# Batch 14's rotation and the first weight split on the other side of a stage boundary, and three scale loads in the attention

## The reference

```python
x = x + jnp.tanh(g_xattn[0]) * _L0_xattn_ref(_layernorm(x, axis=-1), ctx_2048, ctx_2048)
x = x + jnp.tanh(g_ffn[0]) * _L0_ffn_ref(_layernorm(x, axis=-1), L0_ffn_SU_ug, L0_ffn_SU_dp, ...)
...
# _L0_ffn_ref, SCALE = 64, INTER = 2048
x = fwht(x * SU_ug) / SCALE
x_up = x @ W_up.T * (Wscale_ug[:INTER] * SCALE)
x_gate = x @ W_gate.T * (Wscale_ug[INTER:] * SCALE)
x = jax.nn.silu(x_gate) * x_up
x = fwht(x * SU_dp) / SCALE
x = x @ W_down.T * (Wscale_dp * SCALE)
```

## Time and profile before

| what | value |
|---|---|
| median of 3 runs | 2079.65 us (2076.43 to 2081.3) |
| profiled execution | 2077.13 us, span 2075.4 us |
| PE busy | 2005.1 us (97%) |
| DVE, ACT, POOL busy | 1238.7, 1159.2, 825.6 us |
| mean granted clock of TensorE | 0.986 |

### The profile page before, as it was taken

How to read it: one execution, slowest core, us unless ns; L and a number is a source line. 1 busy time by engine, 2 the same in 40 slices (tenths; PEclk the granted TensorE clock), 3 DMA queues, 4 the chain that set the end, 5 groups by cost and what they waited for, 6 DMA issues and landing times. The chain is left out here.

```text
span 2075.4 us, 37475 instructions
## 1 busy us (share of the span) xinstructions
PE 2005.1 (97%) x13368; PEld 1677.3 (81%) x13368; DVE 1238.7 (60%) x2346; ACT 1159.2 (56%) x3063; POOL 825.6 (40%) x997
## 2 busy tenths in 40 slices
PE   8999999999989999999979997899999999899998
PEld 6877777777768888898868886899999999778886
DVE  6766666666644543565445555666666666466665
ACT  5666666666643333353333345777777777355544
POOL 3526436445321000000003445888888787022222
PEclk9999999999999999999999998999999999999999
DMA  5536446454275210203003435333333333311101
GB/s 178 151 96 191 121 132 203 120 153 142 86 216 194 79 61 1 71 1 117 1 26 107 121 116 147 87 96 99 114 97 107 98 104 89 120 57 52 31 28 37
DMA packets 199368, 210.08 MB, mean 101 GB/s; under 512 B 65677, under 2 KB 139853, under 8 KB 198685
## 3 DMA queue, kind: packets, MB, share of 16 engines
q1 hardware_dynamic: 199197, 207.83, 33.1%
HBM read 128.13 MB, written 79.66 MB: 100 GB/s over the span
## 5 line engine op out<-in xcount | busy, mean ns | idle before, releaser
L1815 POOL TENSOR_TENSOR qd_rows<-qd_rows,c_rsum 112x375 f32<-112x375 f32 x256 | 202.2, 811 | 90.2 <-DVE c_rsum L1945 83.2
L1951 DVE TENSOR_TENSOR c_pT_lo<-c_turned,c_pT_hi 125x336 fp32r<-125x336 f32 x256 | 128.4, 502 | 135.2 <-ACT c_pT_hi L1890 135.0
L1881 ACT ACTIVATE qd_rows<-c_score,c_nmax 112x375 f32<-112x375 f32 x256 | 147.1, 575 | 86.7 <-DVE c_nmax L1940 86.7
L1262 ACT ACTIVATE b_silu<-b_gate,b_ug_scale 128x512 f32<-128x512 f32 (+1 forms) x64 | 40.7, 636 | 245.9 <-PE b_up L1384 245.8
L1323 DVE SCALAR_TENSOR_TENSOR b_hidden<-b_up,b_ug_scale,b_silu 128x512 f32<-128x512 f32 (+1 forms) x64 | 43.7, 683 | 197.9 <-ACT b_silu L1262 197.9
L518 ACT ACTIVATE a_probs<-a_score,a_nmax 112x375 f32<-112x375 f32 x256 | 144.5, 575 | 3.1 <-DVE a_nmax L678 3.0
L2229 POOL TENSOR_TENSOR f_probs<-f_probs,f_rsum 112x448 f32<-112x448 f32 x64 | 59.7, 933 | 212.1 <-DVE f_rsum L2350 212.1
L928 PEld LDWEIGHTS a_turned<-keep_ident,a_probs 112*125 112x125 f32 x768 | 110.4, 188 | 35.5 <-issue 22.6
L1940 DVE TENSOR_REDUCE c_nmax<-c_score 112x1 f32<-112x375 f32 x256 | 137.5, 537 | 0.4 <-PE c_score L2021 0.4
L928 PE MATMUL a_turned<-keep_ident,a_probs 112*125 112x112 f32 x768 | 133.8, 283 | 1.5 <-DVE a_pT L684 1.0
L1241 POOL TENSOR_TENSOR ab_zT<-ab_zT,keep_ln_eps 128x1 f32<-128x1 f32 x1 | 0.2, 189 | 310.5 <-DVE ab_zT L1352 310.5
(11 more groups left out here) (335 smaller groups left out, 6079.6 us busy)
## 6 DMA issues: line engine op xcount, KB each, us to landing
q<-q_qT SPq DMA_DIRECT2D x14, 1024.0 KB
qd_raws<-q SPq DMA_DIRECT2D x64, 224.0 KB, 4.5
k<-bq_raw SPq DMA_DIRECT2D x16, 752.0 KB, 4.1
qd_raws<-k SPq DMA_DIRECT2D x64, 188.0 KB, 3.3
v<-bq_raw SPq DMA_DIRECT2D x48, 250.0 KB
qd_raws<-v SPq DMA_DIRECT2D x64, 187.5 KB
bq_raw<-in_ctx_dram SPq DMA_DIRECT2D x15, 672.0 KB
wug<-a_ug_turned SPq DMA_DIRECT2D x32, 256.0 KB, 2.3
```

Of the source, the lines that this page charges most:

```text
L1815: pool.tensor_tensor(probs[:, n % AHEAD, :], probs[:, n % AHEAD, :], rsum[:, n % (2 * H):n % (2 * H) + 1].broadcast_to([S, T]), ALU.mult). ...
L1881: act.activation(probs[:, n % AHEAD, :], score[n % AHEAD][0:S, 0:T], ACT.Exp, bias=nmax[:, c:c + 1], accum_out=sums[:, c:c + 1]).then_inc( ...
L1951: dve.tensor_tensor(pT[1][:, t % 2, :, j, :], src, f32(pT[0][:, t % 2, :, j, :]), ALU.subtract).then_inc(pT_split, 1)
```

## The change

The tail of phase_a no longer turns, copies, rotates, splits and stores batch 14. In phase_b TensorE starts with the four transposes of its z (into `y[3]`), ACT copies them after its first weight split, TensorE multiplies by the Hadamard matrix behind `project(0)` (into `y[2]`), ACT and DVE split the result within step 0, and `reduce(0)` waits for that. SP stores it after all weights, ahead of `load_turned(1)`. The split of weight chunk 0 moves from phase_b into phase_a's tail (b = 16, n = 0), on ACT ahead of `keys_out(15, 2)`, on DVE ahead of `gated(15)`. The buffers `wu` and of the scales move into `ab`. The three scale loads move into phase_a, at b = 8, behind `load_first` and ahead of batch 9's list. The diff, cut to its core:

```diff
             def load_first():
...
+            def load_scales():
+                with nc.allow_non_contiguous_dma(reason="scales by partition"):
+                    sp.dma_start(ab["ug_scale"][:, :], io["Wscale_ug"].rearrange("(c p) -> p c", p=P)).then_inc(ab["scales_loaded"], 16)
+                    sp.dma_start(ab["down_signs"][:, :], io["SU_dp"].rearrange("(c p) -> p c", p=P)).then_inc(ab["scales_loaded"], 16)
+                row = io["Wscale_dp"].rearrange("(a n) -> a n", a=1)
+                sp.dma_start(ab["down_scale"][:, :], row.broadcast_to([P, D])).then_inc(ab["scales_loaded"], 16)
...
-                if b >= 2:
+                if 2 <= b < B:
                     store_rotated(b - 2)
                 if b == B // 2:
                     load_first()
+                    load_scales()
...
+            for n in range(2):
+                sp.wait_ge(lead_loaded[n], 32)
+            sp.wait_ge(ab["scales_loaded"], 48)
...
+            def lead_weights_hi():
+                act.wait_ge(lead_loaded[0], 32)
+                act.activation(ab["wu"][0][:, 0, :, :, :], lead_weights, ACT.Copy).then_inc(lead_hi, 1)
...
+                    if n == 0 and b == B:
+                        lead_weights_hi()
                     if n == 0 and before:
                         keys_out(b - 1, 2)
...
-                    if n == 5 and b >= 2:
+                    if n == 5 and b >= 2 and cur:
                         copy_z(b - 2)
...
+                    if n == 0 and b == B:
+                        dve.wait_ge(lead_hi, 1)
+                        dve.tensor_tensor(ab["wu"][1][:, 0, :, :, :], lead_weights, f32(ab["wu"][0][:, 0, :, :, :]), ALU.subtract)
                     if n == 1 and before:
                         gated(b - 1)
...
-            with nc.allow_non_contiguous_dma(reason="scales by partition"):
-                sp.dma_start(ug_scale[:, :], ...
             for c in range(LEAD, 4):
                 load_weights(c)
...
             load_x(0)
+            sp.wait_ge(early_split, 1)
+            store_rotated(final - 1)
             load_turned(1)
...
-            for t in range(2):
-                weights_hi(t)
-            act.wait_ge(scales_loaded, 48)
+            weights_hi(1)
+            act.wait_ge(early_turned, 1)
+            act.activation(zT[:, :], y[3][:, 0:DC * S], ACT.Copy).then_inc(early_copied, 1)
...
+                if t == 0:
+                    act.wait_ge(early_rotated, 1)
+                    act.wait_ge(ab["xr_stored"], 32 * (final - 1))
+                    act.activation(xr[0][:, :, :], y[2][:, 0:DC * S].rearrange("p (c s) -> p c s", c=DC), ACT.Copy,
+                                   scale=float(D) ** -0.5).then_inc(early_hi, 1)
...
+            for c in range(DC):
+                last = pe.transpose(y[3][:, c * S:(c + 1) * S], z[:, 0, c * P:(c + 1) * P], keep["ident"][0:S, 0:S])
+            last.then_inc(early_turned, 1)
             project(0)
+            pe.wait_ge(early_copied, 1)
+            pe.matmul(y[2][:, 0:DC * S], keep["hadamard"][:, :], zT[:, :], start=True, stop=True).then_inc(early_rotated, 1)
```

More of the change, by code:

```diff
@@ L136, in first_layer @@
             "xr": [m.sb(f"xr_{n}", [P, DC, S], F32R) for n in ("hi", "lo")],
+            "wu": [m.sb(f"wu_{n}", [P, 2, 2, DC, P], F32R) for n in ("hi", "lo")],
+            "down_scale": m.sb("down_scale", [P, D]),
+            "down_signs": m.sb("down_signs", [P, IC]),
+            "ug_scale": m.sb("ug_scale", [P, 2 * IC]),
             "v_stored": [m.sem(f"v_stored{n}") for n in range(KC)],
         }
-        for name in ("x_stored", "k_stored", "xr_stored", "xres_loaded"):
+        for name in ("x_stored", "k_stored", "xr_stored", "xres_loaded", "scales_loaded"):
             ab[name] = m.sem(name)
@@ L205, in phase_a @@
         kout = stage[:, STAGE_V:].rearrange("p (c t) -> p c t", c=DC)
+        lead_weights = ab["lead"][:, B % CTX, 0:2 * D].rearrange("p (n d k) -> p n d k", n=2, d=DC)
         def sems(*names):
@@ L217, in phase_a @@
         ctx_loaded = [m.sem(f"ctx_loaded{n}") for n in range(CTX)]
-        lead_loaded, first_loaded = sems("lead_loaded", "first_loaded")
+        lead_loaded = [m.sem(f"lead_loaded{n}") for n in range(2)]
+        first_loaded, lead_hi = sems("first_loaded", "lead_hi")
         x_counted, x_moments, x_shifted, x_scaled, xn_done = sems("x_counted", "x_moments", "x_shifted", "x_scaled", "xn_done")
@@ L255, in phase_a @@
             out_uses += [("queries", b + 1, 0)] if after else []
-            out_uses += [("z", b - 2, 0)] if b >= 2 else []
+            out_uses += [("z", b - 2, 0)] if b >= 2 and cur else []
             out_uses += [("job", b, 5), ("weigh", b, 2), ("keys", b, 1), ("job", b, 7)] if cur else []
@@ L363, in load_lead @@
                 sp.wait_ge(down_stored, 16 * 13)
-                sp.dma_start(ab["lead"][:, (B + c) % CTX, 0:2 * D].rearrange("p (n d) -> p n d", n=2), io["wug"][c, :, :, :]).then_inc(lead_loaded, 16)
-                sp.dma_start(ab["lead"][:, (B + c) % CTX, 2 * D:3 * D], io["wdn"][c, :, :]).then_inc(lead_loaded, 16)
+                sp.dma_start(ab["lead"][:, (B + c) % CTX, 0:2 * D].rearrange("p (n d) -> p n d", n=2), io["wug"][c, :, :, :]).then_inc(lead_loaded[c], 16)
+                sp.dma_start(ab["lead"][:, (B + c) % CTX, 2 * D:3 * D], io["wdn"][c, :, :]).then_inc(lead_loaded[c], 16)
+            def load_scales():
[4 more added lines that the diff above has]
+                sp.dma_start(ab["down_scale"][:, :], row.broadcast_to([P, D])).then_inc(ab["scales_loaded"], 16)
             def load_first():
@@ L608, in _ @@
                         ctx_hi(b + 1, 2)
-                    if n == 6 and b >= 2:
+                    if n == 6 and b >= 2 and cur:
                         rotated_hi(b - 2)
@@ L977, in rotate_z @@
                 pe.wait_ge(z_copied, b + 1)
[L978 to L981, removed]
+                pe.wait_ge(v_out, KC * (b + 2) + 2)
                 pe.wait_ge(hadamard_made, 2 * HADAMARD_STAGES)
@@ L1083, in phase_b @@
     xres, tmp, signs, z, zT, xr = (ab[name] for name in ("xres", "tmp", "signs", "z", "zT", "xr"))
+    wu, down_scale, down_signs, ug_scale, scales_loaded = (ab[name] for name in ("wu", "down_scale", "down_signs", "ug_scale", "scales_loaded"))
     with Memory(nc, "b") as m:
@@ L1114, in phase_b @@
             m.sem(n) for n in ("next_loaded", "next_counted", "next_moments", "next_shifted", "next_scaled", "next_hi"))
-        scales_loaded, signed, scale_done = (m.sem(n) for n in ("scales_loaded", "signed", "scale_done"))
+        signed, scale_done = m.sem("signed"), m.sem("scale_done")
+        early_turned, early_copied, early_rotated, early_hi, early_split = (
+            m.sem(n) for n in ("early_turned", "early_copied", "early_rotated", "early_hi", "early_split"))
         wu_hi, wu_split, wd_hi, wd_split = m.sem("wu_hi"), m.sem("wu_split"), m.sem("wd_hi"), m.sem("wd_split")
@@ L1159, in load_x, with store_rotated @@
                 sp.dma_start(xio[:, 0:TILES[g], :], x1[:, first_tile[g]:first_tile[g + 1], :]).then_inc(x_loaded, 16)
+            def store_rotated(b):
+                for n in range(2):
+                    sp.dma_start(io["xt"][n, :, :, b * S:(b + 1) * S], f32(xr[n][:, :, :])).then_inc(ab["xr_stored"], 16)
             def store_ordered(c):
@@ L1181, in _ @@
             load_x(0)
+            sp.wait_ge(early_split, 1)
+            store_rotated(final - 1)
             load_turned(1)
             sp.wait_ge(xr_split, 1)
-            for n in range(2):
-                sp.dma_start(io["xt"][n, :, :, final * S:B * S], f32(xr[n][:, :, :])).then_inc(ab["xr_stored"], 16)
+            store_rotated(final)
             sp.wait_ge(ab["k_stored"], 16 * B)
@@ L1311, in order_weights @@
                     dve.copy_predicated(columns(n, slice(DS, HD)), swap[:, :, :], low[:, 1 - n, :, :]).then_inc(wa_done, 1)
-            for t in range(2):
-                weights_lo(t)
-            dve.wait_ge(scales_loaded, 48)
+            weights_lo(1)
             dve.tensor_tensor(ug_scale[:, 0:IC], ug_scale[:, 0:IC], down_signs[:, :], ALU.mult).then_inc(signed, 1)
@@ L1326, in _ @@
                 dve.tensor_tensor(wd[1][:, p, :], down_chunk(c), f32(wd[0][:, p, :]), ALU.subtract).then_inc(wd_split, 1)
+                if t == 0:
+                    dve.wait_ge(early_hi, 1)
+                    dve.scalar_tensor_tensor(out=xr[1][:, :, :], in0=y[2][:, 0:DC * S].rearrange("p (c s) -> p c s", c=DC),
+                                             scalar=float(D) ** -0.5, in1=f32(xr[0][:, :, :]), op0=ALU.mult, op1=ALU.subtract).then_inc(early_split, 1)
                 dve.wait_ge(h_hi, t + 1)
@@ L1336, in _ @@
                 if t == 1:
+                    dve.wait_ge(early_turned, 1)
                     dve.wait_ge(x1_scaled, 1)
@@ L1373, in project @@
                 g, c, p, width = place(t)
-                pe.wait_ge(wu_split, t + 1)
+                if t:
+                    pe.wait_ge(wu_split, t)
```

(2 more changed lines are left out.)

12 lines of the change are left out of this document (2 added, 10 removed).

## The result

The changed kernel takes 2085.05 us (median of 9 runs, 2083.17 to 2086.4), the kernel before 2078.33 (median of 9, 2076.43 to 2081.65). The ratio is 1.003 with a 95% interval of 1.002 to 1.0041: 6.7 us slower. The forecast was 2077.5, 2.1 us faster than the 2079.65 known then, so size and sign are wrong. The profiled execution took 2086.40, 9.3 us more than the profiled one of before.

A forecast was written before the change was run, and what follows sets the result against it. TensorE, busy 97% of the span, was taken as the bound. A handover gain of 4.1 us less 2.0 for the scale loads gave 2.1 off 2079.65, so 2077.5 us; range 2074.4 to 2081.3.

The forecast's parts named there:

- The scale loads' price: Middle of the attention: word loads delay batch 8's residual and so TensorE; 2.0 us lost, bounds 0 and 4.
- If SP also is held: Middle of the attention: second scale issue holds SP, residual issued near 347 us, landing near 350.5; TensorE 2.5 late.
- TensorE loses L − 347.9: Batch 9 of the attention: TensorE's loss in us when batch 8's residual load lands at time L.
- The boundary sum: Handover from attention to feed-forward: all gains and losses there together, 4.1 us gained, bounds 3.4 and 5.8.
- The stage's start: Handover: without batch 14's tail SP is free at 595.84 instead of 598.69; 2.85 us gained.
- The transposes: Start of the feed-forward stage: four transposes of z come first on TensorE; 0.7 us lost, between 0.4 and 1.1.
- Step 0's chain: Feed-forward step 0: batch 14's copy and subtraction make the hidden chain about 0.5 us later; cost nothing, 1.2 cover remaining.
- the credit of 0.35 for the clock: First projection: if the transposes count toward the slow-clock stretch, the projection has 0.7 less of it, gaining 0.35 us.
- C: Rival, middle of the attention: word loads hold SP one after the other; 6 us slower, 2085.7; chance 0.08.
- A: Rival, middle of the attention: the scale loads are hidden, the whole 4.1 us is gained, 2075.5; chance 0.20.
- B: Rival, handover: the clock stays up through the shorter pause, 1.7 us more gain, 2075.8; chance 0.08.
- D: Rival, handover: late ACT, DVE or lead load sets the end, or rotation stalls; gain 2, total 2079.6; chance 0.14.

The follow-up runs named there:

- x1_place: The kernel before with only the split-weight and scale buffers moved, no work moved: 2085.45 us against 2077.9, ratio 1.0034.
- x2_pad: The changed kernel with 320 unused bytes per partition ahead of the feed-forward stage's own buffers: 2077.22 us, 0.9993 of the kernel before.
- x3_quiet: The changed kernel with the three scale loads issued in batch 10, behind the load of x: 2080.26 us, 1.0014 of the kernel before.
- m7_resfirst: x2_pad with the scale loads behind batch 8's residual load instead of ahead of it: 2078.32 us, 1.0003 of the kernel before.
- x4_both: The changed kernel with the 320 unused bytes and the scale loads in batch 10: 2073.92 us against 2077.9, ratio 0.9982.
- m6_hand: x4_both with the first weights' split behind the keys' copy on ACT and the gated product on DVE: 2075.18 us, 0.9985 of the kernel before.

## Why the prediction was wrong

**What failed first: a part of the change that was not priced.** The prediction's list has the turn, the split, the scale loads, and each wait; the front part says that `wu` and the scale buffers move, and the working gives this no term at all. It is the largest one: 6.4 us in the profile, 7.5 in the medians of x1_place alone, 7.8 back in x2_pad. The three scale buffers have 2048, 64 and 128 bytes, and the last two take all that comes behind them 192 bytes off the common offset. A pace of 0.227 us a matmul of 512 columns in before was a sign that nothing held up TensorE; it was not a sign that this would stay.

**The scale loads' price was mis-sized: 2.0 taken, 5.2 in the profile** (4.8 between the medians of the changed kernel and x3_quiet). The chain was the right one, and its steps came out by their numbers. "If SP also is held ... lands near 350.5": it was, the landing was 351.55. "TensorE loses L − 347.9": 3.65, measured 3.59. Three things were short. I took a value between SP not held (1.3) and held (2.5), where the earlier trace rows already showed SP held for 2.66 us in such an issue; and even the held case let the residual land 3.5 us after its issue near 347, where it was issued at 346.05 and took 5.5. And I priced the pause alone, not the clock behind it, 1.5 us, though the earlier trace rows had shown what a pause does. m7_resfirst corrects the mechanism as well: what costs is SP, held 7 to 8 us with everything behind it, and not this one load. That the residual can't overtake the words is not tested by these runs; SP's held issue came first. The section "Queues, rings and completion order" of the page "DMA: Bandwidth & Descriptors" of the Trainium skill, cited for it, has the order for the taking of descriptors only: a later write may finish before an earlier one.

**The boundary sum was right, in part by luck.** 4.1 forecast, 4.0 in the medians (x4_both against before), 4.1 in its profile. The stage's start: 2.85 forecast, 3.8 in x4_both. The weights' wait: gone, 2.42. The transposes: 0.66 for 0.7. Step 0's chain and the later stores: nothing waits, as priced. Wrong was the credit of 0.35 for the clock: the first projection took 0.7 more than before in x4_both, not less. So in x4_both the start gives 0.95 more than its term and the clock takes 1.05 more than its own, and the two cancel. Five traces have this same handover, and their gains differ: 2.65 in the changed kernel (start 2.6, projection 0.9 longer), 3.2 in m7_resfirst, 3.6 in x3_quiet, 4.0 in x2_pad (start 2.9, projection 0.1 shorter), 4.1 in x4_both.

**The rivals.** C came out at 2085.7, close to the measured 2085.05, by a sum that is wrong: the word loads do hold SP, but the third issue took 0.97 and the residual landed at 351.6, not 358; its middle costs 5.2 and not 10, and the rest is the buffers. A is refuted by the pause, B by the clock. In D, ACT and DVE do end last in the changed kernel (DVE at 601.5, 0.3 us behind the landing that SP waits for, the start 1.3 later), at a price of some tenths, not 2.

## What to carry to other kernels

Price the allocation as a part of the change: a small buffer put ahead of big ones shifts every matmul operand behind it, so keep those operands' offsets as they were (or, for matmuls of 512 columns, equal within 256 bytes), with some unused bytes if need be, and compare the matmul pace where the edit has changed nothing. A load of single words behind another one held the queue that issues it for 2.7 to 7.9 us here, longest behind 2 MB under way. Put it where nothing behind it is due, and ask for everything behind it, not only for the first transfer. Add to every new pause of TensorE the slow clock behind it.

## What the runs showed of the hardware that was not expected

- TensorE's pace with 512-column float32r matmuls depends on where its operands start: 16.32 us for 72 of them (0.2267 each) with equal offsets within 256 bytes, 16.56 to 16.69 for two steps with others, without any recorded wait. With 256 columns the same distances came out the other way (8.52 against 8.37 and 8.43). What inside the chip does this is left open; the runs show only the offsets, and for the down product only that its operands at 0, beside the others at 64 within 256, cost 0.11 for two steps.
- The issue of a DMA of single words, each time right behind a similar one, took 2.66 us at the handover, 4.01 in a quiet stretch of the attention, and 6.92 and 7.85 with 2 MB under way.
- After TensorE's restart at the handover the granted clock came back 3.5 us later in before, and in the changed handover 3.9 (x2_pad), 5.6 (x4_both) and 6 us later (the changed kernel). After the pause of 3.6 us in batch 9 it was at 0.50 for about 3.4 us.
- The same instructions do not start alike in each execution. In the first 26 us m6_hand's trace falls 3.4 us behind before's and x4_both's gets 0.6 ahead, though the two have the same instructions there; that is the whole difference between these two spans (2074.7 and 2070.7).
